# One-hot blocks split between VectorE and GpSimd, and three experts gathered ahead in place of five

## The reference

```python
k = int(CAPACITY_FACTOR * N / E)              # N = 4096 tokens, E = 8 experts, k = 512
xf = x.reshape(N, D)                          # D = 128
route_prob = jax.nn.softmax(xf @ Ws + bs, axis=-1).T
route_vals, routes = jax.lax.top_k(route_prob, k)
xin = xf[routes]
h = jax.nn.gelu(jnp.einsum('ekd,edf->ekf', xin, W1) + b1[:, None, :])   # f = 512
out = jnp.einsum('ekf,efd->ekd', h, W2) + b2[:, None, :]
out = out * route_vals[..., None]
final = jnp.zeros((N, D), dtype=x.dtype).at[routes.reshape(-1)].add(out.reshape(-1, D))
```

## Time and profile before

| | us |
|---|---|
| median of 3 runs | 4461.14 |
| lowest and highest | 4453.69, 4463.28 |
| the profiled execution | 4456.33 |
| its span in the profile | 4454.5 |
| PE busy | 3964.2 |
| DVE busy | 3584.2 |
| ACT busy | 2960.2 |
| POOL busy | 2206.9 |

### The profile page before, as it was taken

The page is one execution under the profiler, slowest core; times in us unless marked ns, Lnnn a source line. Parts: engine busy times, 40 slices in busy tenths (PEclk is TensorE's granted clock), DMA queues, the critical chain, the costliest instruction groups (busy, mean ns, idle before and its releaser), DMA issues. The chain is left out here.

```text
span 4454.5 us, 117888 instructions
## 1 busy us (share of the span) xinstructions
PE 3964.2 (89%) x43247; PEld 2386.8 (54%) x43247; DVE 3584.2 (80%) x8496; ACT 2960.2 (66%) x5496; POOL 2206.9 (50%) x1392
## 2 busy tenths in 40 slices
PE   8978999999999999999999999999999855737735
PEld 5644555555555555555555555555555533525534
DVE  6887999899998999989999899989999655356341
ACT  3425787787777777777787787777778545636402
POOL 0005666666666666666666666666666400130006
PEclk9989999999999999999999999999999966868658
DMA  1012232333233332233232332232323200000102
GB/s 43 1 40 65 66 68 64 83 68 69 65 69 82 69 70 65 65 84 70 65 68 64 83 73 64 64 85 65 70 64 68 50 15 12 1 5 18 72 7 37
DMA packets 188120, 251.24 MB, mean 56 GB/s; under 512 B 88676, under 2 KB 129382, under 8 KB 187366
## 3 DMA queue, kind: packets, MB, share of 16 engines
q1 hardware_dynamic: 182054, 240.47, 23.2%
q0 software_dynamic: 5632, 4.33, 0.7%
HBM read 41.65 MB, written 14.30 MB: 13 GB/s over the span
## 5 line engine op out<-in xcount | busy, mean ns | idle before, releaser
L1419 POOL TENSOR_TENSOR f_rot_a<-f_rot_a,f_rot_b 128x1024 f32<-128x1024 f32 x384 | 908.1, 2370 | 311.8 <-DVE f_rot_b L1160 206.6
L1427 POOL TENSOR_TENSOR f_rot_a<-f_rot_a,f_norm 128x1024 f32<-128x1024 f32 x384 | 731.3, 1905 | 648.5 <-DVE f_norm L1178 525.4
L844 PE MATMUL f_bank<-f_w_vo,f_xs_t 128*32 128x512 f32 x6144 | 815.8, 603 | 0.2
L1157 DVE TENSOR_TENSOR f_rot_a<-f_bank,f_rot 128x512 f32<-128x512 f32 x768 | 523.0, 682 | 76.2 <-ACT f_squares L1519 40.4
L1528 ACT ACTIVATE f_vo<-f_bank 128x512 f32<-128x512 f32 x768 | 458.6, 597 | 170.2 <-PE f_bank L844 162.6
L1519 ACT ACTIVATE f_squares<-f_bank 128x512 f32<-128x512 f32 x768 | 455.8, 594 | 113.1 <-PE f_bank L830 67.1
L1540 ACT ACTIVATE f_k_t<-f_bank 64x512 f32<-64x512 f32 x768 | 452.7, 589 | 102.7 <-PE f_bank L866 98.2
L1160 DVE TENSOR_TENSOR f_rot_b<-f_bank,f_rot 128x512 f32<-128x512 f32 x768 | 505.9, 674 | 0.0
L1433 POOL TENSOR_TENSOR f_prob<-f_score,f_stat 128x512 f32<-128x512 f32 x384 | 400.6, 1043 | 192.1 <-DVE f_stat L1210 187.7
L1164 DVE TENSOR_REDUCE f_sums<-f_squares 128x16 f32<-128x1024 f32 x384 | 464.5, 1210 | 4.7 <-ACT f_squares L1519 4.7
L876 PEld LDWEIGHTS f_bank<-f_k_t,f_q_t 128*32 128x32 f32 x12288 | 345.4, 110 | 179.4 <-issue 99.5
(11 more groups left out here) (446 smaller groups left out, 7372.8 us busy)
## 6 DMA issues: line engine op xcount, KB each, us to landing
f_vo_off<-f_vo SPq DMA_DIRECT2D x1152, 128.0 KB, 2.3
f_vo_off<-f_vo SPq DMA_DIRECT2D x384, 64.0 KB, 2.0
f_w_qk<-in_Wqk SPq DMA_DIRECT2D x12, 512.0 KB, 5.3
f_vo_dram<-f_vo_pair SPq DMA_DIRECT2D x48, 128.0 KB, 1.8
f_x_shifted<-s_all SPq DMA_DIRECT2D x48, 128.0 KB
f_x_shifted<-s_all SPq DMA_DIRECT2D x48, 127.0 KB
f_w_vo<-f_vo_dram SPq DMA_DIRECT2D x10, 512.0 KB, 5.4
e_w<-in_e_W SPq DMA_DIRECT2D x2, 2048.0 KB, 12.7
```

The lines of the kernel that those rows point to most:

```text
L844: done = nc.tensor.matmul(bank[V][32 * w:32 * w + 32, :], x[:, at:at + 32], w_vo[:, 4 * g:4 * g + 4, w // 2, :], start=True, stop=True)
L1157: nc.vector.tensor_tensor(rot_a[:, slot, n, :].rearrange("p (h d) -> p h d", h=GROUP), source, c_tab, ALU.mult)
L1419: nc.gpsimd.tensor_tensor(rot_a[:, slot, :, :], rot_a[:, slot, :, :], rot_b[:, g, :, :], ALU.add).then_inc(rot_summed, 1)
L1427: nc.gpsimd.tensor_tensor(heads, heads, over(norm[:, 16 * g:16 * g + 16], [128, 16, HEAD_DIM]), ALU.mult).then_inc(qk_normed, 1)
```

## The change

Two edits. The 16 row blocks move from VectorE's list to GpSimd's, behind a new wait on `low_made`; VectorE marks `low` as made with an instruction that does nothing else. And `RING` goes from 5 to 3.

```diff
@@ choose, GpSimd @@
             nc.gpsimd.tensor_copy(tile_no[:, :, :], over(counts[:, 0:TILES], shape)).then_inc(tile_numbered, 1)
+            pool.wait_ge(tile_numbered, 1)
+            pool.wait_ge(low_made, 1)
+            for n in range(LOW):
+                nc.gpsimd.tensor_scalar(placed[:, 1, n, :, :], low[:, :, :], float(n + 1), counts[:, TILES:TILES + 1], ALU.is_equal, ALU.mult).then_inc(row_placed, 1)
@@ choose, VectorE @@
-            dve.wait_ge(counts_in, 16)
+            nc.vector.nop().then_inc(low_made, 1)
             dve.wait_ge(tile_numbered, 1)
             for n in range(LOW):
                 nc.vector.scalar_tensor_tensor(placed[:, 0, n, :, :], low[:, :, :], float(n + 1), tile_no[:, :, :], ALU.is_equal, ALU.mult).then_inc(tile_placed, 1)
-            for n in range(LOW):
-                nc.vector.tensor_scalar(placed[:, 1, n, :, :], low[:, :, :], float(n + 1), counts[:, TILES:TILES + 1], ALU.is_equal, ALU.mult).then_inc(row_placed, 1)
             for n in range(HIGH):
@@ apply_experts @@
-    RING, PARTS = 5, CAPACITY // 128
+    RING, PARTS = 3, CAPACITY // 128
```

## The result

| | median us | lowest to highest | runs |
|---|---|---|---|
| before | 4462.13 | 4453.69 to 4463.58 | 6 |
| changed | 4479.41 | 4475.66 to 4480.81 | 6 |

The ratio is 1.0039, with a 95% interval of 1.0029 to 1.0049: the change makes the kernel slower by 17.3 us (13 to 22). The forecast was 4479. That the two lie within half a microsecond of each other is luck: one term was 4.6 us too small, and a gain of 7 us was not foreseen.

The account below looks back on a forecast made before the run. GpSimd, issuing indirect DMAs, was taken to bound the experts stage and VectorE choose. Row blocks +4.2 and ring +14.3 made +18.5 us on 4456.33, 4474.8; the runs' median stands 4.8 higher, giving 4479, range 4465 to 4486.

Parts of the forecast that it names:

- The ring: In the experts stage, RING 3 leaves GpSimd idle before the first rows and makes later rows late: +14.3 us.
- The row blocks: In choose, moving 16 row blocks to GpSimd delays TensorE's sorting, as VectorE and GpSimd exclude each other: +4.2 us.
- S(2) - S(0): In the experts stage, time from the scatter start of expert 0 to that of expert 2: 27.1 us.
- R: In the experts stage, time from an expert's turn to the rows of the expert before it: taken as 12.3 us.
- so I take 0.46: In choose, the price in us of one row block on GpSimd; 16 of them 7.4 us.
- the two lists add up: In choose, full exclusion makes VectorE's 9.91 us and GpSimd's 7.4 sum to 17.3 against 13.05.
- The library load: In choose, the GpSimd library load that the row blocks bring costs nothing, at most 6.4 us.
- no exclusion: Rival: in choose GpSimd's blocks fit between VectorE's, -3.1 us; with the ring +11.2, 4472; chance 0.18.
- both together: Rival: no exclusion in choose and full clock in the experts stage, +5.5 us, 4467, counted as none; chance 0.08.
- Clock stays up: Rival: in the experts stage TensorE keeps full clock, ring +8.6 us; in all +12.8, 4474; chance 0.13.
- Other side: Rival: two open waits in the experts stage and 3.1 us in choose go, 7.9 us faster, 4453; chance 0.03.
- Dearer still: Rival: GpSimd blocks in choose 0.60 us each, R 12.6, later gathers landing late: +25 us, 4486; chance 0.10.

Follow-up runs that it names:

- e1_ring: Kernel before with only RING cut from 5 to 3, all row blocks still on VectorE: 4475.84 us against 4462.71, ratio 1.0029.
- e8_clock: As e1_ring, plus unused TensorE products, 8 before the turn of expert 3 and 4 before those of 4 to 7: 4469.96 us, ratio 1.0020 to before.
- e11_ring4: Kernel before with four experts gathered ahead in place of five: one run at 4463.3 us.
- e3_probe: Kernel before plus 28 GpSimd operations of 128 x 256 into unread scratch, four of each of seven forms; one run, no time given, S(7) - S(0) 76.58 us.
- e12_other: Kernel before plus an unused GpSimd tensor_scalar, then an unused partition_all_reduce that loads the other library again: 4461.71 us against 4463.17, ratio 0.9999.
- e6_split: Changed kernel with GpSimd making 6 of the 16 row blocks, VectorE the other 10, and RING at 5: ratio 0.9985 to before.
- e7_spread: Kernel before with its 12 later gathers in threes behind four scatters, not fours behind three: 4465.01 us against 4465.78, ratio 0.9997.
- e10_both: Kernel before plus an unused GpSimd tensor_scalar, and the later gathers in threes as in e7_spread: 4453.05 us, ratio 0.9981.

## Why the prediction was right, and where it was not

The ring was priced rightly and for the right reasons. The row blocks and the start of the program were not, and their errors happened to cancel.

**The ring, +14.3: right in mechanism and size.** Measured +14.2 in the changed kernel and 13.5 in e1_ring. Its parts, S(2) - S(0), S(4) - S(2), S(6) - S(4), were given as 27.1 each and are 26.77, 27.07 and 27.16, the last step 9.53 against 9.59. Three small terms were off and cancel in part. A scatter released by DVE's `rows` starts 0.3 us behind them, not 0.75: in the chain, `rows` end at about 4372.27 and the scatter starts at 4372.55. I had taken 0.75 from a scatter released by a landing. The turn starts 2.54 us behind its gather, not 2.66. And R is 12.57 to 12.95, not 12.3: the turn of 3 is at 4386.48 and the last of DVE's rows ends at 4399.05. The restarted clock stayed low for 5.6 to 6.0 us (until about 4392.1, 4419.4 and 4446.3), longer than in the quicker of the two restarts from which 12.3 was taken. This part varies from run to run: in e1_ring it was 4.7 us behind the turn of 3 (from 4380.9 to about 4385.6), and S(2) - S(0) is 26.38 there. S(0) came 25.53 us behind the first gather and not 25.07 (25.32 - 0.25), since the first product took 6.49 us at the start of the stage against 5.58. The idle stretch ahead of the first scatter, given as about 9 us, is 10.5, and by the prediction's own rows it should have read 10.0 (from 4351.9 to 4361.9). The share that I gave the clock was nearly right: with the clock up the forecast was S(7) - S(0) = 85.1, and e8_clock has 84.69.

**The row blocks, +4.2: the direction right, the reason wrong.** Measured +8.8. The step that failed is "so I take 0.46": the price was bounded by a cast and half a tensor_tensor, neither of which compares. It measured 1.14 alone and 1.38 beside VectorE. Sixteen of these take 21.6 us, the short gaps between them counted, longer than VectorE's list, so GpSimd became the bound. The second step that failed is the exclusion taken from the earlier trace rows for all 48 blocks: "the two lists add up" would have made VectorE's two groups take 9.9 us plus GpSimd's; they grew from 9.9 to 12.0. Here I set the rule of the Trainium skill ("SBUF — State Buffer", "Who interferes with whom") against the rows again: for float32 tensor_tensors the whole-instruction block is what the earlier trace rows show, for these short bf16 operations it is not, and the measurement decides. With the true price of the operation and full exclusion the stage would have come to 9.9 + 16 x 1.14 = 28.1 us; it came to 21.8.

**The library load, "costs nothing": right where it stands, wrong for the program.** At 4254.8 it was covered by a wait of 57 us. But it changes what the next execution finds, and is worth -7.2 us at its start. No row of one profile alone could show that; the row that could have raised the question is the idle stretch of 7.67 us with "issue" ahead of the first affine_select, which looks like the earlier trace rows. The prediction's own sign of error, that anything before 4310 moves, did come.

So the total was met by a ring that was right, 4.6 us too little in one place and 7.2 too much in another. That the two errors are nearly the same size is luck. The forecast was also added to the 4461.1 us of three runs of before, and the six have 4462.1.

Of the rivals, "no exclusion" (-3.1) and "both together" fail on the price of the operation: even with no exclusion at all GpSimd's 16 operations would take 18.3 us. "Clock stays up" is what e8_clock made true. "Other side" needed sooner rows of expert 0, which came no sooner. "Dearer still" was nearest to what the two edits do where they stand: it had +6.5 and 15.2 + 3 for them, and 8.8 and 14.2 were measured, 23 us in all. Without the gain at the start the time would have been some 4486 us, where that rival stood.

## What to carry to other kernels

How far to run ahead is set by the first consumer. Gathers that are issued while the first result is being made cost nothing here. Those taken out of that time are paid for later (3.4 us for the first four in e11_ring4, 10.1 for the next four in e1_ring), and the more so if the engine behind then idles into its slow clock. Moving work to an idle engine needs the price of that very operation there; if no row has it, put four of each candidate form into a stretch in which the engine waits, and read them from one profile. And look at the first ten microseconds too: in these runs, where one execution of a program follows another, the kernels that end in the GpSimd library with which they begin save a load of some 7 us.

## What the runs showed of the hardware that was not expected

- On GpSimd an is_equal over 128 x 256 costs 0.85 us, where mult and add together cost 0.40 (e3_probe). For compare and mult the data type makes no difference (1136 and 1142 ns), and VectorE does the two in 0.20 us, from start to start.
- The GpSimd library appears to stay loaded from one execution to the next: the same load instruction stands at 1.3 us in the kernel before and at 1.5 in the changed one, and is followed by 7 us of idleness or by none, by the library loaded last. That it survives is inferred from this; what happens when another program runs in between was not tried.
- An affine_select does not seem to need that load. In `choose` of the kernel before the same kind of operation (line 3438) runs at 4252.3 us, behind the load of the other library for partition_all_reduce at 3999.6 and with no load in between; in e12_other it starts 0.16 us behind a memset. Whether the first load can be left out was not tried.
- In the three profiles that were taken on one chip (e3_probe, e6_split, e7_spread, and no other) the stretch from the first gather to S(0) is 30.2 us in place of 25. TensorE's transposes for expert 2 are torn apart there by idle time that ends with nothing the profile shows, as in e7_spread:

```profile
4364.06 0.27 PE L3612 MATMUL ea_t_bank<-ident,ea_taken 128*128 128x128 f32 x1
4365.07 0.38 PE L3612 MATMUL ea_t_bank<-ident,ea_taken 128*128 128x128 f32 x2 [0.74 <-issue]
4367.86 0.27 PE L3612 MATMUL ea_t_bank<-ident,ea_taken 128*128 128x128 f32 x1 [2.42 <-issue]
```

The edits don't explain it (e10_both has the edit of e7_spread, and 25.44). The median of before on that chip, 4465.78 us, is 2.6 to 3.9 us above those on the others (4461.87 to 4463.17), so it may be the chip's, but before was not profiled there, and the cause stays open. What is concluded from these three above rests on other stretches of them, or on the before of that chip.
